# One load of the input on SyncE's queue, or sixteen indexed loads by GpSimd

## The chip, the cores and the metric

The kernel runs on one core of a Trainium2 chip. Its time is the device time of the whole program in microseconds (us), and less is better. The core has TensorE (PE in the profile, with PEld for its weight loads), VectorE (DVE), ScalarE (ACT), GpSimd (POOL) and SyncE (SP), which run side by side, each in the order of its own program, and wait for each other through semaphores. Transfers between the chip's main memory (HBM) and the on-chip memory are issued by one of these engines and carried out by 16 DMA engines. The before kernel took 1201.54, 1200.2 and 1196.77 us in three runs, a median of 1200.2.

## The reference

The program is a decoder of two layers on an input `x` of 8 batches, 256 positions and 128 features in float32, with a context of 8 x 64 rows:

```
x = layernorm(x + attention_16_heads(x))      # causal
x = layernorm(x + linear_cross_attention(x, ctx))
x = layernorm(x + mixture_of_experts_16(x))
x = layernorm(x + gated_recurrence(x))
x = layernorm(x + cross_attention(ctx, x))
x = layernorm(x + mixture_of_experts_64(x))
```

Only the first line matters here. `x` enters it twice: transposed, features on partitions, as the operand of the matrix products, and by rows, positions on partitions, as the term to which the attention's result is added (the residual).

## The kernel before

The 2048 rows of `x` are seen as T = 16 tiles of 128. The host lays them out as `a["x"]`, of shape (128, 16, 128): partition, tile, feature; one partition's data are 8 KB that lie together. On the chip they are held in `X`, a view of `Xp` behind a pad of 256 columns. The transposed copy is `xall`, filled from `a["xT"]`.

SyncE's program (from L374) begins with a row of loads, issued one behind the other without a wait: the context and its weights, the four attention weights `w64v`, `w64o`, `w64q`, `w64k` (512 KB each), `xall` (1 MB, L380), `X` (1 MB, L381), and then the small weights that later stages use.

GpSimd's program (from L417) clears and fills constants, squares a context tile once VectorE has made it (L442), waits for `kn_sum` from VectorE, raises `kn` to the power -0.5 (L444), and enters the main loop. There its part is `divide` (L454), which scales a tile of probabilities by a reciprocal that VectorE has computed.

TensorE first makes context products (L1397, L1404, L1410, L1418) and folds the attention weights into products (L1387, eight groups); ScalarE and VectorE take their results out of PSUM (L627, L871). Then the main loop runs 4 x 16 steps over batches and head pairs. In every step TensorE waits for `Ul`, the low part of a product that VectorE rounds (L940), before it can go on to the scores.

VectorE's order is what counts for the change. Behind its setup stand the clearing of two PSUM banks (L897), the low part of `wq` (L899), the split of the first router's weights (L902, L904), and the wait for `X` (L906). Directly behind that wait the loop begins: `mask_and_max` (L912, L915) reads the scores of the step before, then `Ul` (L940), the copy of the transposed probabilities (L927), in some steps `add_out` (L933), which is the first instruction that reads or writes the data of `X`, and the reciprocals (L922). The waiting instruction is thus ahead of all of VectorE's work of the loop:

```
dve.wait_ge(sem("x_in"), 16)
```

The order is written out by hand for every engine; there is no planner.

Of the kernel before, what the change touches and what calls it, by code (L numbers as in the profile page):

```python
# [19 lines left out]
ACT = mybir.ActivationFunctionType  # L20
AX = mybir.AxisListType
F32 = mybir.dt.float32
# [4 lines left out]
N = B * S  # L27
T = N // 128
# [13 lines left out]
def decoder_program(nc, a, out):  # L42
# [14 lines left out]
    def sb(name, shape, dt=F32, scope=ctx):  # L57
        return scope.enter_context(nc.sbuf_tensor(name, shape, dt))

    with ctx:  # L60
# [13 lines left out]
        cmask = sb("cmask", [128, 2 * 128])  # L74
        ones = sb("ones", [128, 128])
        scratch = sb("scratch", [128, 24])
        st = sb("st", [128, T, 6])
        mv = sb("mv", [128, T, 2])
        rs = sb("rs", [128, T])
# [292 lines left out]
        @block.sync  # L372
        def _(sp):
            sp.dma_start(ctxT[:, :], a["ctxT"]).then_inc(sem("ctx_in"), 16)  # L374
            sp.dma_start(wx[:, :, :], a["wx"]).then_inc(sem("ctx_in"), 16)
            sp.dma_start(brow[:, :], a["brow"]).then_inc(sem("ctx_in"), 16)
            sp.dma_start(bq[:, :], a["bq"]).then_inc(sem("ctx_in"), 16)
            for n in "voqk":
                sp.dma_start(w64[n][:, :, :], a["w64" + n]).then_inc(sem("w_vo_in" if n in "vo" else "w_qk_in"), 16)
            sp.dma_start(xall[:, 0:N], a["xT"]).then_inc(sem("xT_in"), 16)  # L380
            sp.dma_start(X, a["x"]).then_inc(sem("x_in"), 16)  # L381
            sp.dma_start(wr_in[:, :], a["wr0"]).then_inc(sem("wr_in"), 16)
            for name, dst in (("wd", wd_in), ("abias", abias), ("wo1", wo1), ("wqe", wqe), ("wr1", wr1_in),
                              ("ebias", ebias), ("wsh", wsh)):
                sp.dma_start(dst[tuple([slice(None)] * len(dst.shape))], a[name]).then_inc(sem("l1_in"), 16)

            sp.wait_ge(sem("x_added"), NC_)
            sp.dma_start(rw[:, :], a["rw"]).then_inc(sem("rw_in"), 16)
            with sp.Fori(0, E0 // 2) as i:
                for s in range(2):  # L390
                    sp.wait_ge(sem("w_split"), i * 2 + s + 2)
                    sp.dma_start(W0[s][:, :], a["w12"][ds(i * 2 + s, 1), :, :].rearrange("o p n -> p (o n)")).then_inc(sem(f"w_in{s}"), 16)

            sp.wait_ge(sem("r_step"), 8)
            sp.dma_start(decay, wu[:, 0, :]).then_inc(sem("decay_out"), 16)
            sp.wait_ge(sem("decay_out"), 16)
            by_batch = decay.rearrange("(h b) t -> b h t", b=B)
            for g in range(B):
                if g >= 2:
                    sp.wait_ge(sem("scan1_done"), 2 * g - 2)  # L400
                sp.dma_start(Wb[g % 2][:, :].rearrange("p (h t) -> p h t", h=H1),
                             by_batch[g:g + 1, :, :].to_broadcast([128, H1, S])).then_inc(sem(f"decay_in{g % 2}"), 16)

            sp.wait_ge(sem("x_added"), NC_ + NC_)
            with sp.Fori(0, E1 // 4) as i:
                for s in range(2):
                    sp.wait_ge(sem("f_split"), i * 2 + s + 1)
                    sp.dma_start(W3[s][:, :], a["w3"][ds(i * 2 + s, 1), :, :].rearrange("o p n -> p (o n)")).then_inc(sem(f"w_in{s}"), 16)
            for c in range(NC_):
                sp.wait_ge(sem("ln_x"), 5 * T + 4 * c + 4)  # L410
                sp.dma_start(out[:, 4 * c:4 * c + 4, :], X[:, 4 * c:4 * c + 4, :]).then_inc(sem("out_done"), 16)
            sp.wait_ge(sem("out_done"), 16 * NC_)

        @block.gpsimd
        def _(pool):
# [3 lines left out]
            pool.memset(cmask[:, :], 0.0).then_inc(sem("zeroed"), 1)  # L419
            pool.memset(ones[:, :], 1.0).then_inc(sem("consts"), 1)  # L420
            pool.memset(neghalf[:, :], -0.5).then_inc(sem("consts"), 1)
            pool.memset(wrh[:, :].bitcast(F32), 0.0).then_inc(sem("wr_zero"), 1)
            pool.memset(wrl[:, :].bitcast(F32), 0.0).then_inc(sem("wr_zero"), 1)
            pool.wait_ge(sem("zeroed"), 3)
            pool.affine_select(out=ident[:, :], in_=ident[:, :], compare_op=ALU.not_equal, fill=1.0,
                               base=0, pattern=[[-1, 128]], channel_multiplier=1).then_inc(sem("consts"), 1)
# [5 lines left out]
            pool.affine_select(out=blockones[:, :], in_=blockones[:, :], compare_op=ALU.is_ge, fill=0.0,  # L432
                               base=DX - 1, pattern=[[DX, HX], [0, DX]], channel_multiplier=-1).then_inc(sem("consts"), 1)

            pool.memset(xall[:, N:], 0.0).then_inc(sem("x_pad"), 1)
            pool.memset(P[:, 2, :], 0.0).then_inc(sem("norm_done"), 1)
            pool.memset(PT[:, 1, :, :], 0.0).then_inc(sem("pt_done"), 1)
            pool.memset(VO[:, :, :, :], 0.0).then_inc(sem("vo_done"), 1)
# [4 lines left out]
            pool.wait_ge(sem("ctx_dve"), CTX_DVE["kn_sum"])  # L443
            pool.tensor_tensor(kn[:, :], kn[:, :], neghalf[:, 0:B], ALU.pow).then_inc(sem("ctx_pool"), 1)  # L444


            def divide(g, k):

# [169 lines left out]
        def _(act):  # L618
# [12 lines left out]
                               ACT.Copy).then_inc(sem("xh_done"), 1)  # L631

            act.wait_ge(sem("xT_in"), 16)
            act.wait_ge(sem("x_pad"), 1)
            split_x(0, 0)
            act.wait_ge(sem("ctx_pool"), CTX_POOL["kn_done"])
            act.wait_ge(sem("ctx_pe"), CTX_PE["g2_ready"])
# [28 lines left out]


            for c in range(NC_):
                act.wait_ge(sem("q_ready"), c + 1)
                act.activation(EQ[:, c * CH:c * CH + CH], bank(4 + c), ACT.Exp, bias=bq[:, 0:1]).then_inc(sem("q_act"), 1)  # L670

            for c in range(NC_):
                act.wait_ge(sem("q_norm"), c + 1)
                act.activation(RQ[:, c * CH:c * CH + CH], bank(c), ACT.Ln, scale=float(DX)).then_inc(sem("q_act"), 1)
            for c in range(NC_):
                act.wait_ge(sem("q_act"), NC_ + c + 1)
# [111 lines left out]
                act.activation(XTf[:, c * CH:c * CH + CH], bank(c), ACT.Copy).then_inc(sem("ln_hi"), 1)  # L788
            for h in range(2):
                act.wait_ge(sem("es_step"), 6 + 2 * h)  # L790
                act.activation(SE[:, 8 * h:8 * h + 8, :], SE[:, 8 * h:8 * h + 8, :], ACT.Exp).then_inc(sem("e_exp"), 1)
            for c in range(NC_):
                act.wait_ge(sem("e_T"), c + 1)
                act.activation(PE_T[:, c * CH:c * CH + CH], bank(c)[0:64, :], ACT.Copy).then_inc(sem("e_pt"), 1)
            in_turn(lambda c: ln_norm(act, 4, c), lambda c: ln_hi(act, 4, c), 1)

            for c in range(NC_):
# [51 lines left out]

        @block.vector  # L850
        def _(dve):
            dve.wait_ge(sem("consts"), 5)
            dve.memset(sel2[:, 64:72].bitcast(F32), 0.0)
            dve.tensor_tensor(sel2[:, 0:64], ident[:, 0:64], ident[:, 64:128], ALU.add).then_inc(sem("sel2_done"), 1)
            dve.tensor_reduce(halfones[:, :], ident[:, :].rearrange("p (a c) -> p a c", a=2), AX.X, ALU.add).then_inc(sem("halves"), 1)
# [42 lines left out]
            dve.wait_ge(sem("ctx_act"), CTX_ACT["wq_hi"])  # L898
            dve.tensor_tensor(wql[:, :], wx[:, 3, :], wqh[:, :].bitcast(F32), ALU.subtract).then_inc(sem("ctx_dve"), 1)  # L899
            dve.wait_ge(sem("wr_in"), 16)  # L900
            dve.wait_ge(sem("wr_zero"), 2)
            dve.tensor_copy(wrh[:, 0:E0R], wr_in[:, :]).then_inc(sem("ctx_dve"), 1)  # L902
            dve.wait_ge(sem("ctx_dve"), CTX_DVE["wr_split"] - 1)
            dve.tensor_tensor(wrl[:, 0:E0R], wr_in[:, :], wrh[:, 0:E0R].bitcast(F32), ALU.subtract).then_inc(sem("ctx_dve"), 1)  # L904

            dve.wait_ge(sem("x_in"), 16)  # L906

            def mask_and_max(g, k):

# [91 lines left out]
                dve.tensor_tensor(x, x, bank(b), ALU.add).then_inc(sem("x_added"), 1)  # L1001

            def add_query_out(c):
                dve.wait_ge(sem("b_out"), c + 1)
                dve.wait_ge(sem("bo_added"), c + 1)
                add_bank(c, 4 + c)
                dve.wait_ge(sem("x_added"), c + 1)
                ln_stats(dve, 1, c)
# [246 lines left out]
            row_reduce(1, 5, ALU.max)  # L1255
            less_maximum(1, 7)
            for h in range(2):
                dve.wait_ge(sem("e_exp"), h + 1)
                row_reduce(h, 8, ALU.add)
            for h in range(2):  # L1260
                dve.wait_ge(sem("es_step"), 9 + h)
                dve.reciprocal(el[:, 8 * h:8 * h + 8], em[:, 8 * h:8 * h + 8]).then_inc(sem("es_step"), 1)
            for c in range(NC_):
                dve.wait_ge(sem("e_out"), c + 1)
                add_bank(c, 4 + c)
                dve.wait_ge(sem("x_added"), NC_ + c + 1)
                ln_stats(dve, 4, c)
# [106 lines left out]
        def _(pe):  # L1374
# [15 lines left out]


            pe.wait_ge(sem("ctx_in"), 64)
            pe.wait_ge(sem("consts"), 5)
            for n in range(2):
                for p in range(4):
                    dst = bank(n)[:, p * 128:p * 128 + 128]
# [52 lines left out]
                last.then_inc(sem("pv_done"), 1)  # L1449

            pe.wait_ge(sem("fold_lo"), 8)
            pe.wait_ge(sem("consts"), 5)
            pe.wait_ge(sem("acc_free"), 1)
            with pe.Fori(0, B // 2) as i:
                for k in range(STEPS):
# [25 lines left out]
            def project_query(c):  # L1481
                cc = slice(c * CH, c * CH + CH)
                pe.wait_ge(sem("ln_lo"), c + 1)
                mm3(bank(4 + c), (wqh[:, :], wql[:, :]), (XTh[:, cc], XTl[:, cc])).then_inc(sem("q_ready"), 1)

            pe.wait_ge(sem("ctx_dve"), CTX_DVE["wq_lo"])
            in_turn(lambda c: ln_transpose(pe, 0, c), project_query, 2)
            for c in range(NC_):
                pe.wait_ge(sem("q_sq"), c + 1)
                pe.matmul(bank(c), blockones[:, :], SQ[:, c * CH:c * CH + CH], start=True, stop=True).then_inc(sem("q_norm"), 1)  # L1490
            for c in range(NC_):
                pe.wait_ge(sem("q_done"), c + 1)
                for t in tiles(c):
                    dst = bank(4 + c)[:, t % 4 * 128:t % 4 * 128 + 128]
                    last = pe.matmul(dst, Q[:, t * 128:t * 128 + 128], G2[:, t // 2, :], start=True, stop=True)
                last.then_inc(sem("b_out"), 1)


            def gate_logits(c):
# [180 lines left out]
            for t in range(T):  # L1680
                pe.wait_ge(sem("e_prob"), t // 8 + 1)
                last = pe.transpose(bank(t // 4)[0:64, t % 4 * 128:t % 4 * 128 + 128], SE[:, t, :], ident[:, :])
                if t % 4 == 3:
                    last.then_inc(sem("e_T"), 1)
            for t in range(T):
                pe.wait_ge(sem("e_pt"), t // 4 + 1)
                last = pe.matmul(bank(4 + t // 4)[:, t % 4 * 128:t % 4 * 128 + 128], PE_T[:, t * 128:t * 128 + 128], vE[:, t // 2, :],
                                 start=True, stop=True)
                if t % 4 == 3:
                    last.then_inc(sem("e_out"), 1)  # L1690

            def router_logits(c):
                cc = slice(c * CH, c * CH + CH)
# [141 lines left out]
```

## Time and profile before

| | us |
|---|---|
| median of three runs (lowest, highest) | 1200.2 (1196.77, 1201.54) |
| profiled execution: its time | 1198.43 |
| profiled execution: its span, first to last instruction | 1196.7 |
| PE busy | 1059.1 (88%) |
| DVE busy | 886.8 (74%) |
| ACT busy | 678.7 (57%) |
| POOL busy | 426.1 (36%) |
| mean granted TensorE clock, as a share of the full one | 0.922 |

The profile shows one execution, whose time is 1.7 us above its span. Busy shares are means over stages with different limits, so the stretch around the change is to be read by itself: the setup, up to about 35 us, and the start of the main loop, which lasts until about 340 us. Instructions that issue a DMA on SyncE's or GpSimd's queue are not counted as busy; their times stand in the timeline.

### The profile page before, as it was taken

To read this page: it belongs to the slowest core of one execution; us is meant where nothing else is said; L and a number is where in the kernel's file an instruction comes from. 1 tells how busy PE (TensorE), PEld (TensorE's weight loads), DVE (VectorE), ACT (ScalarE), POOL (GpSimd) and SP (SyncE) were. 2 spreads that over 40 slices of the span, in tenths; PEclk is the share of its full clock that TensorE was granted. 3 is DMA by queue.
4 is the path that set the end of the run, shared out by engine and by line. 5 is a ranking of instruction groups with operands and counts; after the bars stand their busy time and mean duration, and the time that the engine had idled before them with its cause. 6 is when DMAs were issued, how large, how long until landed. Compare 5 with 4: busy or idle time off the path is not lost. (4 is left out here: it accounts for less than half of the span.)

```text
span 1196.7 us, 18412 instructions
## 1 busy us (share of the span) xinstructions
PE 1059.1 (88%) x5684; PEld 890.0 (74%) x5684; DVE 886.8 (74%) x2063; ACT 678.7 (57%) x1513; POOL 426.1 (36%) x517
## 2 busy tenths in 40 slices
PE   7899999999966799999897178877869999999995
PEld 7899999999844588888675068875637888888883
DVE  3566666666674789898768599954868888888885
ACT  2666666666665777777688243434634444444444
POOL 3233333333345223232216076753542223222232
PEclk7999999999986899999989578896969999999998
DMA  7000000000000000000000355400000000000000
GB/s 209 1 2 1 0 0 0 0 0 0 0 1 19 18 18 26 18 26 18 1 0 1 62 100 76 48 1 1 28 0 27 20 20 20 21 25 20 20 13 35
DMA packets 18263, 26.70 MB, mean 22 GB/s; under 512 B 1905, under 2 KB 14769, under 8 KB 17714
## 3 DMA queue, kind: packets, MB, share of 16 engines
q1 hardware_dynamic: 18226, 26.24, 10.0%
q8 instruction: 19, 0.31, 0.1%
q14 instruction: 18, 0.15, 0.0%
HBM read 25.12 MB, written 1.11 MB: 22 GB/s over the span
## 5 line engine op out<-in xcount | busy, mean ns | idle before, releaser
L454 POOL TENSOR_TENSOR P<-P,rl 128x256 f32<-128x256 f32 (+1 forms) x130 | 104.8, 827 | 204.9 <-DVE rl L922 204.9
L841 ACT ACTIVATE FG<-PS 128x512 f32<-128x512 f32 x120 | 71.8, 598 | 146.0 <-PE PS L1378 146.0
L915 DVE CUSTOM_DVE_ANT_0 P<-PS,cmask 128x128 f32<-128x128 f32 (+1 forms) x260 | 77.1, 352 | 70.9 <-issue 70.9
L1363 DVE TENSOR_TENSOR FU<-FG,PS 128x512 f32<-128x512 f32 x120 | 82.5, 688 | 49.9 <-PE PS L1378 49.9
L647 ACT ACTIVATE P<-P,mn 128x128 f32<-128x128 f32 (+1 forms) x260 | 114.3, 444 | 2.4 <-DVE mn L915 2.4
L559 POOL TENSOR_TENSOR W3h<-W,ones 128x384 fp32r<-128x384 f32 x32 | 39.3, 1229 | 212.4 <-PE PS L1378 209.6
L704 ACT ACTIVATE SG<-PS 128x512 f32<-128x512 f32 x128 | 76.4, 598 | 46.5 <-PE PS L1378 31.0
L1377 PE MATMUL PS<-XTl,W3h 128*128 128x512 f32 x256 | 101.8, 397 | 0.0
L1376 PE MATMUL PS<-XTh,W3h 128*128 128x512 f32 x256 | 101.3, 396 | 0.4
L1378 PE MATMUL PS<-XTh,W3l 128*128 128x512 f32 x256 | 101.2, 395 | 0.0
L1446 PE MATMUL PS<-VO,PT 128*128 128x128 f32 x804 | 100.6, 275 | 0.0
L1087 DVE TENSOR_TENSOR HL<-Hf,HH 128x512 fp32r<-128x512 f32 x128 | 98.3, 768 | 0.7
L1446 PEld LDWEIGHTS PS<-VO,PT 128*128 128x128 f32 x804 | 95.0, 192 | 0.0
L1346 DVE TENSOR_TENSOR FHL<-FH,FHH 128x512 fp32r<-128x512 f32 x128 | 91.6, 716 | 0.7 <-ACT FHH L831 0.7
L1104 DVE TENSOR_TENSOR Hf<-SG,PS 128x512 f32<-128x512 f32 x112 | 76.8, 685 | 16.5 <-PE PS L1558 16.0
L831 ACT ACTIVATE FHH<-FH 128x512 fp32r<-128x512 f32 x128 | 80.0, 625 | 9.0 <-DVE FH L1355 7.5
L699 ACT ACTIVATE HH<-Hf 128x512 fp32r<-128x512 f32 x128 | 79.7, 623 | 4.0 <-DVE Hf L1092 3.7
L1367 DVE TENSOR_TENSOR FH<-FU,PS 128x512 f32<-128x512 f32 x120 | 81.5, 680 | 0.0
L655 ACT ACTIVATE Uh<-PS 128x512 fp32r<-128x512 f32 x64 | 38.3, 598 | 72.2 <-PE PS L1378 72.2
L927 DVE COPY PT<-PS 128x768 f32<-128x768 f32 x66 | 62.5, 947 | 2.9 <-PE PS L1435 2.9
L1376 PEld LDWEIGHTS PS<-XTh,W3h 128*128 128x128 f32 x256 | 48.1, 188 | 14.8 <-issue 2.9
L1435 PE MATMUL PS<-ident,P 128*128 128x128 f32 x396 | 56.3, 278 | 2.1 <-POOL P L454 2.1
(390 smaller groups left out, 2963.3 us busy)
## 6 DMA issues: line engine op xcount, KB each, us to landing
Wb<-decay SPq DMA_DIRECT2D x8, 1024.0 KB, 14.4
W<-in_w SPq DMA_DIRECT2D x32, 192.0 KB, 2.3
W<-in_w SPq DMA_DIRECT2D x16, 256.0 KB, 2.6
xall<-in_xT SPq DMA_DIRECT2D x1, 1024.0 KB, 13.6
Xp<-in_x SPq DMA_DIRECT2D x1, 1024.0 KB, 15.5
out<-Xp SPq DMA_DIRECT2D x4, 256.0 KB, 2.3
wd_in<-in_wd SPq DMA_DIRECT2D x1, 832.0 KB
w64v<-in_w64v SPq DMA_DIRECT2D x1, 512.0 KB, 6.0
```

The costliest lines, as they stand in the source:

```text
L454: last = pool.tensor_tensor(v, v, f, ALU.mult)
L647: last = act.activation(P[:, slot, c:c + w], P[:, slot, c:c + w], ACT.Exp, scale=-1.0, bias=mn[:, par, q:q + 1], accum_out=ls[:, par, q:q ...
L699: act.activation(HH[:, (k - 1) % 4, :], Hf[:, (k - 1) % 4, :], ACT.Copy).then_inc(sem("hh_done"), 1)
L831: act.activation(FHH[:, (k - 1) % 4, :], FH[:, (k - 1) % 4, :], ACT.Copy).then_inc(sem("fhh_done"), 1)
L1087: dve.tensor_tensor(HL[:, (k - 1) % 4, :], Hf[:, (k - 1) % 4, :], HH[:, (k - 1) % 4, :].bitcast(F32), ALU.subtract).then_inc(sem("hl_done" ...
L1346: dve.tensor_tensor(FHL[:, (k - 1) % 4, :], FH[:, (k - 1) % 4, :], FHH[:, (k - 1) % 4, :].bitcast(F32), ALU.subtract).then_inc(sem("fhl_do ...
L1363: dve.tensor_tensor(FU[:, k % 2, :], FG[:, k % 2, :], bank(6), ALU.mult).then_inc(sem("ft_done"), 1)
L1367: dve.tensor_tensor(FH[:, k % 4, :], FU[:, k % 2, :], bank(7), ALU.mult).then_inc(sem("fh_done"), 1)
L1376: pe.matmul(dst, l[0], r[0], start=start, stop=False, skip_group_check=skip)
L1377: pe.matmul(dst, l[0], r[1], start=False, stop=False, skip_group_check=skip)
L1378: return pe.matmul(dst, l[1], r[0], start=False, stop=stop, skip_group_check=skip)
L1446: last = pe.matmul(OB[:, dst:dst + 128], PT[:, par, h, blk * 128:blk * 128 + 128], VO[:, half, 2 * p + h, :], start=first, stop=(p == PAIR ...
```

## The change

The one load of `X` goes out of SyncE's program. GpSimd makes a table `xrow` of row numbers, in which partition p holds p*16 + t in column t, and behind its work on `kn`, ahead of the main loop, issues sixteen indexed loads. Load t reads from the table one row number for each partition and fetches that row of 512 bytes, so that it fills tile t. VectorE waits in the same place as before, now for all sixteen.

```diff
+        xrow = sb("xrow", [128, T], mybir.dt.uint32)
...
             sp.dma_start(xall[:, 0:N], a["xT"]).then_inc(sem("xT_in"), 16)
-            sp.dma_start(X, a["x"]).then_inc(sem("x_in"), 16)
             sp.dma_start(wr_in[:, :], a["wr0"]).then_inc(sem("wr_in"), 16)
...
-            pool.memset(wrh[:, :].bitcast(F32), 0.0).then_inc(sem("wr_zero"), 1)
-            pool.memset(wrl[:, :].bitcast(F32), 0.0).then_inc(sem("wr_zero"), 1)
+            pool.memset(wrh[:, :].bitcast(F32), 0.0).then_inc(sem("consts"), 1)
+            pool.memset(wrl[:, :].bitcast(F32), 0.0).then_inc(sem("consts"), 1)
...
-            pool.memset(xall[:, N:], 0.0).then_inc(sem("x_pad"), 1)
+            pool.memset(xall[:, N:], 0.0).then_inc(sem("consts"), 1)
+            pool.iota(xrow[:, :], [[1, T]], base=0, channel_multiplier=T).then_inc(sem("x_rows"), 1)
...
             pool.tensor_tensor(kn[:, :], kn[:, :], neghalf[:, 0:B], ALU.pow).then_inc(sem("ctx_pool"), 1)
+            pool.wait_ge(sem("x_rows"), 1)
+            rows = a["x"].rearrange("p t d -> (p t) d")
+            for t in range(T):
+                pool.indirect_dma_start(out=X[:, t, :], out_offset=None, in_=rows,
+                                        in_offset=bass.IndirectOffsetOnAxis(ap=xrow[:, t:t + 1], axis=0)).then_inc(sem("x_in"), 16)
...
-            act.wait_ge(sem("x_pad"), 1)
+            act.wait_ge(sem("consts"), 8)
...
-            dve.wait_ge(sem("consts"), 5)
+            dve.wait_ge(sem("consts"), 7)
...
-            dve.wait_ge(sem("wr_zero"), 2)
+            dve.wait_ge(sem("consts"), 7)
...
-            dve.wait_ge(sem("x_in"), 16)
+            dve.wait_ge(sem("x_in"), 16 * T)
```

The rest of the diff merges semaphores. `wr_zero` and `x_pad` go into `consts`, as shown; `q_ready`, `q_norm` and `b_out`, all raised by TensorE in the second line of the reference, become one `q_pe`; `e_exp` and `e_pt`, raised by ScalarE, become `e_act`, and `e_T` and `e_out`, raised by TensorE, become `e_pe`. Each wait on one of them is for the count that is reached when the same instruction as before has finished.

## Rows read from the trace of the kernel before

**Rows 1.** Busy time by stage: stage and its length in us, busy us of each engine.

```profile
0.00:34.70 34.70, 26.15 (x144) 25.09 (x144) 11.73 (x25) 9.85 (x21) 10.32 (x21) 0.75 0.64 180
34.70:351.00 316.30, 307.80 (x2171) 279.42 (x2172) 210.34 (x848) 205.49 (x683) 116.08 (x150) 0.98 0.00 0
```

**Rows 2.** Timeline, 29 to 38 us: start us, us, what [idle before it].

```profile
29.21 0.27 DVE L893 MEMSET Xp<- 128x256 f32 x1
...
33.25 0.91 DVE L897 MEMSET PS<- 128x1024 f32 x1 [3.18 <-ACT G L640]
34.07 0.27 DVE L899 TENSOR_TENSOR wql<-wx,wqh 128x128 fp32r<-128x128 f32 x1
34.26 0.16 DVE L902 CAST wrh<-wr_in 128x14 fp32r<-128x14 f32 x1
34.46 0.17 DVE L904 TENSOR_TENSOR wrl<-wr_in,wrh 128x14 fp32r<-128x14 f32 x1
34.68 0.06 DVE L912 MEMSET scratch<- 128x1 f32 x1
...
36.59 0.63 PE L1376 MATMUL PS<-NVh,xh 128*128 128x512 f32 x1 [3.00 <-DVE Ul L940]
...
37.57 1.61 POOL L454 TENSOR_TENSOR P<-P,rl 128x256 f32<-128x256 f32 x2 [16.95 <-DVE rl L922]
```

**Rows 3.** Timeline of POOL and SP in the setup.

```profile
4.83 3.51 POOL L438 MEMSET VO<- 128x4096 f32 x1
...
5.15 0.59 SPq L380 DMA_DIRECT2D xall<-in_xT  x1
5.78 0.50 SPq L381 DMA_DIRECT2D Xp<-in_x  x1
6.32 0.43 SPq L382 DMA_DIRECT2D wr_in<-in_wr  x1
...
10.62 1.04 POOL L442 TENSOR_TENSOR csq<-ck 128x512 f32<-128x512 f32 x1 [2.27 <-DVE ck L863]
...
18.97 1.65 POOL L444 TENSOR_TENSOR kn<-kn,neghalf 128x8 f32<-128x8 f32 x1 [7.31 <-DVE kn L875]
```

**Rows 4.** DMA issues of 0 to 80 us: KB, median us from issue to landing.

```profile
xall<-in_xT SPq DMA_DIRECT2D x1, 1024.0 KB, 13.6
Xp<-in_x SPq DMA_DIRECT2D x1, 1024.0 KB, 15.5
...
w64o<-in_w64o SPq DMA_DIRECT2D x1, 512.0 KB, 7.9
...
wr_in<-in_wr SPq DMA_DIRECT2D x1, 7.0 KB, 15.1
```

**Rows 5.** The chain of waits at 667 us: start us, us, what.

```profile
667.03 1.95 DMA decay<-wu
```

**Rows 6.** POOL's instructions by shape: busy us, mean ns of one | idle before.

```profile
L527 POOL TENSOR_TENSOR gb<-gb,dfb 128x1020 f32<-128x1020 f32 x16 | 37.6, 2352 | 55.8 <-ACT dfb L779 55.8
...
L323 POOL TENSOR_TENSOR rs<-ms,neghalf 128x4 f32<-128x4 f32 x24 | 24.9, 1037 | 2.0
...
L501 POOL CAST esel<-sel 128x128 fp32r x16 | 11.1, 694 | 0.0
...
L560 POOL CAST fsel<-sel 128x128 fp32r x30 | 8.6, 286 | 0.0
...
L482 POOL MEMSET scratch<- 128x1 f32 x1 | 0.1, 98 | 0.0
```

**Rows 7.** Who waited for whom, 0 to 80 us: us, times, longest.

```profile
PE PS L1397 <- DMA bq<-in_bq: 5.9, 1, 5.9
...
PE PS L1387 <- DMA w64o<-in_w64o: 1.6, 1, 1.6
```

**Rows 8.** Stages around the loop's start: columns of Rows 1, then granted clock, DMA share, GB/s.

```profile
26.00:30.00 4.00, 4.00 (x20) 3.78 (x19) 2.40 (x5) 1.34 (x3) 0.00 (x0) 0.50 0.00 0
...
36.00:37.00 1.00, 0.41 (x1) 0.33 (x2) 1.00 (x2) 0.93 (x4) 0.00 (x0) 0.91 0.00 0
37.00:38.00 1.00, 1.00 (x4) 0.78 (x3) 0.49 (x2) 0.00 (x0) 0.43 (x1) 0.50 0.00 0
...
40.00:41.00 1.00, 1.00 (x9) 1.00 (x9) 0.96 (x8) 0.10 (x1) 0.00 (x0) 0.89 0.00 0
41.00:42.00 1.00, 1.00 (x11) 1.00 (x10) 0.71 (x3) 1.00 (x4) 0.00 (x0) 1.00 0.00 0
```

**Rows 9.** Busy time of the stretch in which the new loads begin, columns of Rows 8.

```profile
20.60:34.70 14.10, 12.99 (x74) 12.46 (x72) 7.03 (x15) 5.35 (x14) 0.02 (x1) 0.67 0.25 91
```

More of the change, by code:

```diff
@@ L668, in _ @@
             for c in range(NC_):
-                act.wait_ge(sem("q_ready"), c + 1)
+                act.wait_ge(sem("q_pe"), c + 1)
                 act.activation(EQ[:, c * CH:c * CH + CH], bank(4 + c), ACT.Exp, bias=bq[:, 0:1]).then_inc(sem("q_act"), 1)
             for c in range(NC_):
-                act.wait_ge(sem("q_norm"), c + 1)
+                act.wait_ge(sem("q_pe"), NC_ + c + 1)
                 act.activation(RQ[:, c * CH:c * CH + CH], bank(c), ACT.Ln, scale=float(DX)).then_inc(sem("q_act"), 1)
@@ L790, in _ @@
                 act.wait_ge(sem("es_step"), 6 + 2 * h)
-                act.activation(SE[:, 8 * h:8 * h + 8, :], SE[:, 8 * h:8 * h + 8, :], ACT.Exp).then_inc(sem("e_exp"), 1)
+                act.activation(SE[:, 8 * h:8 * h + 8, :], SE[:, 8 * h:8 * h + 8, :], ACT.Exp).then_inc(sem("e_act"), 1)
             for c in range(NC_):
-                act.wait_ge(sem("e_T"), c + 1)
-                act.activation(PE_T[:, c * CH:c * CH + CH], bank(c)[0:64, :], ACT.Copy).then_inc(sem("e_pt"), 1)
+                act.wait_ge(sem("e_pe"), c + 1)
+                act.activation(PE_T[:, c * CH:c * CH + CH], bank(c)[0:64, :], ACT.Copy).then_inc(sem("e_act"), 1)
             in_turn(lambda c: ln_norm(act, 4, c), lambda c: ln_hi(act, 4, c), 1)
@@ L1003, in add_query_out @@
             def add_query_out(c):
-                dve.wait_ge(sem("b_out"), c + 1)
+                dve.wait_ge(sem("q_pe"), 2 * NC_ + c + 1)
                 dve.wait_ge(sem("bo_added"), c + 1)
@@ L1257, in _ @@
             for h in range(2):
-                dve.wait_ge(sem("e_exp"), h + 1)
+                dve.wait_ge(sem("e_act"), h + 1)
                 row_reduce(h, 8, ALU.add)
@@ L1263, in _ @@
             for c in range(NC_):
-                dve.wait_ge(sem("e_out"), c + 1)
+                dve.wait_ge(sem("e_pe"), NC_ + c + 1)
                 add_bank(c, 4 + c)
@@ L1392, in _ @@
             pe.wait_ge(sem("ctx_in"), 64)
-            pe.wait_ge(sem("consts"), 5)
+            pe.wait_ge(sem("consts"), 7)
             for n in range(2):
@@ L1451, in _ @@
             pe.wait_ge(sem("fold_lo"), 8)
-            pe.wait_ge(sem("consts"), 5)
+            pe.wait_ge(sem("consts"), 7)
             pe.wait_ge(sem("acc_free"), 1)
@@ L1483, in project_query @@
                 pe.wait_ge(sem("ln_lo"), c + 1)
-                mm3(bank(4 + c), (wqh[:, :], wql[:, :]), (XTh[:, cc], XTl[:, cc])).then_inc(sem("q_ready"), 1)
+                mm3(bank(4 + c), (wqh[:, :], wql[:, :]), (XTh[:, cc], XTl[:, cc])).then_inc(sem("q_pe"), 1)
             pe.wait_ge(sem("ctx_dve"), CTX_DVE["wq_lo"])
@@ L1489, in _ @@
                 pe.wait_ge(sem("q_sq"), c + 1)
-                pe.matmul(bank(c), blockones[:, :], SQ[:, c * CH:c * CH + CH], start=True, stop=True).then_inc(sem("q_norm"), 1)
+                pe.matmul(bank(c), blockones[:, :], SQ[:, c * CH:c * CH + CH], start=True, stop=True).then_inc(sem("q_pe"), 1)
             for c in range(NC_):
@@ L1495, in _ @@
                     last = pe.matmul(dst, Q[:, t * 128:t * 128 + 128], G2[:, t // 2, :], start=True, stop=True)
-                last.then_inc(sem("b_out"), 1)
+                last.then_inc(sem("q_pe"), 1)
             def gate_logits(c):
@@ L1683, in _ @@
                 if t % 4 == 3:
-                    last.then_inc(sem("e_T"), 1)
+                    last.then_inc(sem("e_pe"), 1)
             for t in range(T):
-                pe.wait_ge(sem("e_pt"), t // 4 + 1)
+                pe.wait_ge(sem("e_act"), 2 + t // 4 + 1)
                 last = pe.matmul(bank(4 + t // 4)[:, t % 4 * 128:t % 4 * 128 + 128], PE_T[:, t * 128:t * 128 + 128], vE[:, t // 2, :],
@@ L1689, in _ @@
                 if t % 4 == 3:
-                    last.then_inc(sem("e_out"), 1)
+                    last.then_inc(sem("e_pe"), 1)
             def router_logits(c):
```

## The prediction

> **What bounds the kernel now.** I read the stages first. The setup takes 34.7 us. In the attention loop behind it TensorE is busy for 307.8 of 316.3 us while GpSimd has 116.1 us of work [rows 1]. So what reaches the end of the program is TensorE's time, and a later start of the loop is a later end of everything: at 97% busy the loop has no gaps in which TensorE could catch up.
>
> Second, the timeline at the seam, to see what releases the loop. VectorE finishes the split of the router's weights at 34.46 + 0.17 = 34.63 us and begins the loop's first instruction, L912, at 34.68. There is nothing between them: the wait for `X` stands at exactly this place and cost nothing, since `X` had landed at 5.78 + 15.5 = 21.3 us [rows 2 to 4]. TensorE had run out of work and sat idle for 3.0 us until VectorE gave it `Ul` at 36.59 [rows 2]. So at this seam VectorE is the engine on the path, and `X` has a slack of 34.68 - 21.3 = 13.4 us. How late may `X` be? Until 34.68 us for nothing; from there each us of lateness is a us of VectorE, hence of TensorE, hence of the end. That the data are first needed much later, at `add_out`, helps nothing, since the wait is ahead of the loop.
>
> Third, GpSimd's own row of work. Its setup is over at 18.97 + 1.65 = 20.62 us, and it then idles 16.95 us until its first `divide` at 37.57 [rows 2, 3]. The sixteen loads go into this hole. The hole as a whole is 17 us, but what counts is when the last load has landed.
>
> **The change part by part.**
>
> Removed: one issue of 0.50 us on SP and 1 MB from the queue. The loads landed nearly in the order of their issue: `xall` at 5.15 + 13.6 = 18.8, `X` at 21.3, `wr_in` behind it at 6.32 + 15.1 = 21.4 [rows 3, 4]. `X` thus took about 2.5 us of the queue behind everything the setup needs. Later loads come up to 2.5 us earlier, but VectorE reads `wr_in` only at 34.26 [rows 2], 12.8 us after it landed. Gain: 0. The only waits of TensorE for a DMA in the setup are 5.9 us for `bq`, issued ahead of `X`, and 1.6 us for `w64o` [rows 7], which landed at 11.2 us. If `X`, issued at 5.78, shared bandwidth with `w64o`, part of the 1.6 us could come back; that is the bound of the gain, -1.6 us. I take 0, since `X` landed behind the 3.7 MB issued ahead of it.
>
> Added, the table: one iota of 128x16. No iota is in the trace. It stands in front of memsets that end at 4.83 + 3.51 = 8.3 us, and POOL then idles 2.27 us until 10.62 [rows 3]. Even at 1.65 us, the pow over 8 columns and the longest instruction on so few columns, it is inside the idle time. Cost 0; without that cover at most 1.65 us.
>
> Merged semaphores: GpSimd does its instructions in order and each merged count is reached by the same instruction as before. Cost 0; no cover is needed.
>
> Added, the sixteen indexed loads. They begin when POOL is free, at 20.62 us. Let c be the time that POOL spends on one of them, and let the last take 1.95 us from its issue to its semaphore, which is the row of a small transfer that someone waits for [rows 5]. Then `X` is complete at 20.62 + 16c + 1.95, and the loop is late by
>
> D = 20.62 + 16c + 1.95 - 34.68 = 16c - 12.1 us, and 0 where that is below 0.
>
> No row shows c, so it is bounded. From below, SP's issue of a plain load, 0.43 us [rows 3]: 16 x 0.43 = 6.9, D = 0. A gain is excluded but for the 1.6 us above. From above, the longest kind of POOL instruction in the whole trace, 2.35 us on 1020 columns [rows 6]: 16 x 2.35 = 37.6, D = 25.5. Between them lie the pow instructions on few columns, 1.04 us for 4 and 1.65 us for 8 [rows 3, 6]. An indexed load must have GpSimd read 128 row numbers and make a transfer of each, which is more like such an instruction, long for its size, than like an SP issue that says the whole transfer in one step. I take their mean, 1.3 us (an estimate; the middle of the two ends, 1.39, is near it). 16 x 1.3 = 20.8, `X` complete at 43.4, D = 8.7 us. The point that decides: c = 0.76 us gives D = 0, c = 1.13 us gives D = 6.0, which is 0.5%.
>
> The page DMA: Bandwidth & Descriptors of the Trainium skill (Latency and other measured facts) puts the first byte of a DMA issued by GpSimd at about 1 us, which it calls the emission overhead of the cores; by it c would be 1.0, D = 3.9 and the time 1202.3. No row of this trace can check it, as GpSimd issues no DMA here; it names no indexed load of 128 separate rows.
>
> Does something queued behind the loads make it worse? POOL's next instruction is the first `divide`. It needs `rl`, which VectorE makes behind the wait, so it moves to 37.57 + 8.7 = 46.3; POOL has issued its last load at 41.4. It is not late. ScalarE waits for VectorE's minima and TensorE for `Ul`, both moved by D and no more.
>
> TensorE's clock: it idles 3.0 us now and would idle 11.7. After the 3.0 us the granted clock fell to 0.50, its 1.2 GHz level, and the first matmuls of the loop took 0.63 us; at 41 us it was back at 1.00 [rows 2, 8]. After a longer idle the same restart has to be gone through, from the same low level. I count 0. If it took twice as long, some 3.5 us more at half the clock, up to 1.7 us.
>
> VectorE's hold on GpSimd: the same POOL cast of 128x128 takes 286 ns in one stage and 694 ns in another [rows 6], so POOL can be slowed by its neighbours. While the loads begin VectorE is busy 7.0 of 14.1 us [rows 9]; once it waits for `X` it is idle. The bound is that POOL stands still for those 7.0 us; the instructions that copy or clear on-chip data in one stream are L893 and L902, 0.43 us [rows 2]. I take 0, and count up to 1 us for it in the range.
>
> The page SBUF — State Buffer of the Trainium skill (SBUF: two separate sides) says that GpSimd can't write descriptors while VectorE runs a two-port instruction such as a plain copy; by it the sum would grow by those 0.43 us at most, to 1207.5. The unequal casts agree with some such hold but don't show which instructions cause it.
>
> Sum: 0 + 0 + 8.7. Against the profiled execution: 1198.43 + 8.7 = 1207.1 us. That execution lies 1.8 us under the median of the runs; from the median it is 1208.9. I forecast 1208.
>
> **The rivals.**
>
> A, the other side: the issues are cheap and the wait is not, or hardly, felt. Its place is the same wait; it holds from c at or below 1.13 us. For it: 17 us of idle POOL are covered whatever happens, and SP issues a load in 0.43 to 0.59 us [rows 2, 3]. Against it: the index table has to be read and 128 rows handled apart. With c = 0.95, D = 3.1: 1201.5; with c up to 0.76 nothing: 1198.4.
>
> B, the loads are much dearer than one ordinary POOL instruction. If each must land before the next is issued, c = 0.43 + 1.95 = 2.4 us, D = 26: 1224. For it: one semaphore counts all sixteen, and I see no row of many loads out of POOL. Against it: SP issues eighteen loads in a row without waiting for any. If POOL handled the 128 rows one after another at the price of its smallest instruction, 0.098 us [rows 6], c = 12.5 us, D = 188: 1386. Against it: the other POOL instructions handle 128 partitions at once.
>
> The page GPSIMD Engine Reference of the Trainium skill (Performance pitfalls for Q7 kernels) warns of just this, one small read per gather index at about 102 cycles each; at its 1.2 GHz an estimate from it is 10.9 us a load and a time near 1361. Nothing in this trace shows it.
>
> C, faster: the queue without `X` delivers `w64o` earlier, at most -1.6 us, and c is under 0.66 so that `X` isn't late even then: 1196.8. That is inside what counts as no change.
>
> D, the change does not do what it says: the loads could start earlier or later than 20.6. They can't start earlier, since they stand behind the wait for `kn_sum` in POOL's program; a code load ahead of the first would add once. ScalarE's table load at the start of the trace is not of this kind, so I bound it by one long POOL instruction, 2.35 us; it lies within my range.
>
> **How the numbers follow.** The forecast case (c from 1.13 to 2.35, plus small additions) gets 0.50; A 0.36; B 0.11, of which 0.03 for the row-by-row form; C 0.03. What a measurement of this kernel can tell from no change is about 0.5%, 6 us. Slower by more: forecast case and B, 0.61. Within: A and nearly all of C, 0.37. Faster by more: 0.02. The range: at the low end 1200, c = 0.86 from the profiled execution, which leaves out the cheaper half of A and C, some 0.13; at the high end 1227, which takes in the upper bound of c with 2 us of small additions and leaves out 0.07 of B.
>
> **What would show it.** In the new trace: POOL's sixteen issues from about 20.6 us, each 1.3 us long, end near 41.4; the last of `X` lands near 43.4; L912 starts there instead of at 34.68 and its idle time is put down to the DMA; TensorE idles 11 to 12 us ahead of its first matmul on `Ul`; from there to the end the length is unchanged within 2 us. Wrong if L912 still starts near 34.7 (A), if the issues are spaced over 2.3 us (B), or if later stages change length.

## The result, and the profile after

The changed kernel took 1208.31 us (median of four runs, 1206.98 to 1210.07) against 1200.2 for the kernel before, whose fourth run, at 2063.41 us, counts as slow and is left out. The ratio is 1.0075, 95% interval 1.0053 to 1.0098: slower by 8 to 9 us of 1200. The forecast was 1208. The profiled execution has a span of 1205.2 us, 8.5 more than that of before.

By stages, the columns of [rows 1], the changed kernel's start of the loop having moved from 34.7 to 43.05 us:

```profile
0.00:34.70 34.70, 26.16 (x144) 25.09 (x144) 10.36 (x20) 8.88 (x19) 21.13 (x33) 0.75 0.63 169
34.70:43.05 8.35, 0.00 (x0) 0.00 (x0) 1.34 (x4) 1.09 (x3) 5.05 (x5) 0.61 0.16 47
43.05:351.00 307.95, 300.81 (x2149) 276.52 (x2150) 202.58 (x831) 198.24 (x670) 111.76 (x146) 0.98 0.00 0
```

The setup holds the same 26.2 us of TensorE as before [rows 1]. Behind it a stretch of 8.35 us has come in which TensorE does nothing at all. GpSimd's timeline shows what it did in the meantime (start, duration; first and last of sixteen loads, and the first `divide`):

```profile
18.98 1.65 POOL L445 TENSOR_TENSOR kn<-kn,neghalf 128x8 f32<-128x8 f32 x1 [7.46 <-DVE kn L882]
20.83 1.23 POOL L451 DMA_INDIRECT Xp<-in_x,xrow  x1 [0.19 <-issue]
22.36 0.95 POOL L451 DMA_INDIRECT Xp<-in_x,xrow  x1 [0.30 <-issue]
...
36.12 1.26 POOL L451 DMA_INDIRECT Xp<-in_x,xrow  x1 [0.31 <-issue]
...
40.18 0.95 POOL L451 DMA_INDIRECT Xp<-in_x,xrow  x1 [0.30 <-issue]
45.94 1.61 POOL L461 TENSOR_TENSOR P<-P,rl 128x256 f32<-128x256 f32 x2 [4.81 <-DVE rl L929]
```

One load is 0.95 us and 0.30 us of nothing behind it, so 1.25 us from one to the next. The last ends at 41.13. VectorE's timeline, to be held against [rows 2]:

```profile
35.48 0.91 DVE L904 MEMSET PS<- 128x1024 f32 x1 [5.39 <-ACT G L647]
36.30 0.27 DVE L906 TENSOR_TENSOR wql<-wx,wqh 128x128 fp32r<-128x128 f32 x1
36.48 0.16 DVE L909 CAST wrh<-wr_in 128x14 fp32r<-128x14 f32 x1
36.68 0.17 DVE L911 TENSOR_TENSOR wrl<-wr_in,wrh 128x14 fp32r<-128x14 f32 x1
43.05 0.06 DVE L919 MEMSET scratch<- 128x1 f32 x1 [6.20 <-DMA Xp<-in_x,xrow]
```

The first instruction of the loop starts at 43.05, 1.92 us behind the end of the last issue, and waited 6.20 us for the DMA. But the lines above it start 2.2 us later than in [rows 2], before the wait is reached, and that was not forecast. ScalarE and TensorE show more of it:

```profile
33.01 2.18 ACT L647 ACTIVATE G<-PS,kn 128x128 f32<-128x128 f32 x8 [4.54 <-remote]
40.70 0.60 ACT L662 ACTIVATE Uh<-PS 128x512 fp32r<-128x512 f32 x1 [5.51 <-remote]
```

```profile
29.74 0.83 PE L1425 MATMUL PS<-wx,GBT 128*128 128x128 f32 x6
...
31.32 0.28 PE L1385 MATMUL PS<-xh,Ml 128*128 128x256 f32 x1
...
44.96 0.79 PE L1383 MATMUL PS<-NVh,xh 128*128 128x512 f32 x1 [11.36 <-DVE Ul L947]
```

`G` needs L1425, which ended at 30.58, and starts at 33.01. `Uh` needs the product that ended at 31.60, and starts at 40.70. "remote" means that the wait was ended by a semaphore update which the profile can't assign to an instruction near it. In the kernel before the two started at 30.79 and 32.80, within 0.1 us of their inputs or of ScalarE's own work.

Granted clock: before, one stretch at half, of about 3.4 us, from 36.8 to 40.2 [rows 8]; now it lasts from about 36.6 to 50.2 us:

```profile
37.00:40.00 3.00, 0.00 (x0) 0.00 (x0) 0.00 (x0) 0.00 (x0) 2.27 (x3) 0.50 0.15 44
...
46.00:50.00 4.00, 4.00 (x16) 3.61 (x15) 1.20 (x9) 0.75 (x2) 1.55 (x2) 0.50 0.00 0
50.00:51.00 1.00, 1.00 (x10) 1.00 (x9) 0.52 (x1) 1.00 (x4) 0.00 (x0) 0.90 0.00 0
```

The delay followed through the timelines: 8.4 us at the loop's start, 9.1 at the first `add_out` (47.59 to 56.69), 9.3 at the end of the loop (first normalization 335.34 to 344.65), 8.5 at the end of the span.

### The profile page after: what moved, and what is told of

Same layout as the page of the kernel before. It is cut to its first block and busy times, and to the rows that moved or that the text cites. A ratio compares the mean times of both kernels' runs of the same rounds, so it can differ in the third digit from the quotient of the medians.

```text
span 1205.2 us, 18428 instructions
## 1 busy us (share of the span) xinstructions
PE 1061.3 (88%) x5684; PEld 892.4 (74%) x5684; DVE 887.5 (74%) x2063; ACT 679.6 (56%) x1513; POOL 442.2 (37%) x534
## 5 line engine op out<-in xcount | busy, mean ns | idle before, releaser
L711 ACT ACTIVATE SG<-PS 128x512 f32<-128x512 f32 x128 | 76.8, 601 | 48.7 <-PE PS L1385 32.4
L1111 DVE TENSOR_TENSOR Hf<-SG,PS 128x512 f32<-128x512 f32 x112 | 76.7, 684 | 18.5 <-PE PS L1565 17.6
L1383 PEld LDWEIGHTS PS<-XTh,W3h 128*128 128x128 f32 x256 | 48.0, 188 | 13.6 <-issue 2.9
```

The costliest lines, as they stand in the source:

```text
L1383: pe.matmul(dst, l[0], r[0], start=start, stop=False, skip_group_check=skip)
```

## The experiments

All but two are compared in time with the kernel before. For each, three marks of its profiled execution: the start of `kn`, of the loop's first VectorE instruction, and of the first `add_out`. The setup itself comes in two forms, with `kn` at 18.5 to 19.3 us or at 20.3 to 20.8, whatever the kernel (in e10_early `kn` stands behind the loads, and the rest of its setup is of the later form); the low-clock stretch differs too. So each is read against the undisturbed kernel of its own form, before or e1_merges.

| kernel | ratio, interval | kn | loop | add_out |
|---|---|---|---|---|
| before | 1 | 18.97 | 34.68 | 47.59 |
| after | 1.0075, 1.0053 to 1.0098 | 18.98 | 43.05 | 56.69 |
| e1_merges | 1.0004, 0.9991 to 1.0017 | 20.69 | 36.93 | 48.33 |
| e2_late_wait | 1.0081, 1.0063 to 1.0099 | 20.57 | 39.27 | 55.08 |
| e3_half_rows | 1.0106, 1.0088 to 1.0124 | 20.81 | 45.89 | 59.73 |
| e8_eight | 1.0029, 1.0017 to 1.0042 | 20.81 | 38.27 | 51.81 |
| e4_plain_pool | 0.9952, 0.9936 to 0.9969 | 20.32 | 36.57 | 47.97 |
| e5_one_plain_pool | one run, 1203.3 us | 20.60 | 36.24 | 49.15 |
| e6_sp16 | one run, 1199.1 us | 18.94 | 34.88 | 47.78 |
| e7_spread | 1.0025, 1.0005 to 1.0044 | 18.83 | 37.61 | 50.71 |
| e9_plain_32 | 1.0027, 0.9998 to 1.0057 | 19.32 | 35.27 | 48.26 |
| e13_plain_32_wait | 1.0059, 1.0043 to 1.0075 | 20.78 | 41.16 | 54.69 |
| e10_early | 0.9997, 0.9983 to 1.0010 | 28.84 | 36.71 | 49.62 |
| e11_four_late | 1.0036, 1.0025 to 1.0047 | 18.45 | 34.70 | 52.74 |

**The merged semaphores alone.**

```diff
# against the changed kernel
+            sp.dma_start(X, a["x"]).then_inc(sem("x_in"), 16)
-            pool.iota(xrow[:, :], ...)
-            for t in range(T): pool.indirect_dma_start(...)
```

> The changed kernel with its one plain load of X back on SyncE's queue and without index table and indexed loads: only the merged semaphores are left of the change. My theory: the merges cost nothing, ratio 1.000 and the loop's first VectorE instruction at 34.7 us. Rival (the merged counts are reached later, or cost the engines time): up to the whole 1.0075, with a later start of the loop or a longer second line of the reference.

The ratio is 1.0004. VectorE begins the loop at 36.93, not at the forecast 34.7, but `kn` was itself 1.7 us late, and nothing of the change stands ahead of it. By `add_out` the kernel is only 0.7 us behind the kernel before, as TensorE's clock has no low stretch at the loop's start here. The merges show no cost; the interval (0.9991 to 1.0017) leaves room for 2 us at most. This kernel is the mark for the others with the later setup.

**The wait moved to the first use.**

```diff
-            dve.wait_ge(sem("x_in"), 16 * T)
...
             def add_out(b, g):
+                dve.wait_ge(sem("x_in"), 16 * T)
                 dve.wait_ge(sem("pv_done"), g + 1)
```

> All sixteen indexed loads as in the change, but VectorE waits for them only ahead of add_out, its first use of X (47.6 us in the kernel before). My theory (the wait's place turns the loads into time): the 8.4 us go. What is late next is the first divide, behind the last load at 41.1 us: it ends at 42.7 instead of 39.2, and TensorE's second group of transposes starts at about 42.8 instead of 40.6, so about +2 us, ratio 1.002. Rival R (the loads hold up ScalarE: in the changed kernel Uh starts at 40.70 us although its input was ready at 31.6): Uh still starts at 40.7, TensorE's first matmul on NVh at 42 instead of 36.6, +5.4 us, ratio 1.0045. Rival N (the loads disturb nothing and divide has slack): ratio 1.000.

My theory failed: the ratio is 1.0081, as large as with the wait in front. Rival R is seen, though it had been priced at 1.0045. TensorE's product was there at 33.97, and ScalarE and VectorE:

```profile
35.37 2.18 ACT L647 ACTIVATE G<-PS,kn 128x128 f32<-128x128 f32 x8 [5.31 <-issue]
41.76 0.60 ACT L662 ACTIVATE Uh<-PS 128x512 fp32r<-128x512 f32 x1 [4.22 <-remote]
```

```profile
39.27 0.06 DVE L918 MEMSET scratch<- 128x1 f32 x1
...
42.39 0.69 DVE L947 TENSOR_TENSOR Ul<-PS,Uh 128x512 fp32r<-128x512 f32 x1 [1.87 <-issue]
45.36 0.96 DVE L933 COPY PT<-PS 128x768 f32<-128x768 f32 x1 [2.27 <-remote]
```

The loop's VectorE work starts without `X`, and then runs into late signals: `Uh` 7.8 us behind its input, and the copy of the transposes, which TensorE had finished at 34.6, at 45.36. By `add_out` the kernel is 6.8 us behind e1_merges. Two causes lie over each other in the changed kernel, and taking the wait away frees nothing that the time shows.

**Half the rows, half the loads.**

```diff
# e3_half_rows: 16 indexed loads of 64 partitions; the others by SP
-   out=X[:, t, :], ... ap=xrow[:, t:t + 1]
+   out=X[0:64, t, :], ... ap=xrow[0:64, t:t + 1]
# e8_eight: 8 indexed loads of 128 partitions; tiles 0 to 7 by SP
-   for t in range(T):
+   for t in range(T // 2, T):
```

> Sixteen indexed loads of 64 rows instead of 128; the other 64 partitions come by one plain load on SyncE's queue. My theory (the price is of the load, not of the row): spacing of the loads still 1.25 us, the loop starts at 43 us, ratio 1.0075. Rival (the price is of the row): spacing near 0.6 to 0.8 us, last landing at 32 to 35 us, the loop starts at 34.7 to 36, ratio 1.000 to 1.001.

> Eight indexed loads of 128 rows for tiles 8 to 15; tiles 0 to 7 come by one plain load on SyncE's queue. My theory (late = issue start + n x 1.25 + 1.9 us): the last lands at 20.8 + 10 + 1.9 = 32.7 us, before VectorE gets to the wait, ratio 1.000. Rival R (GpSimd's loads hold up ScalarE): VectorE gets to the wait late, as in the changed kernel at 36.9 instead of 34.6, +2 us, ratio 1.002. Rival (a fixed delay of using this kind of load at all): most of the 8.4 us stays, ratio 1.005 or more.

Issues of 64 rows, and of 128 in the second kernel (minimum, median, maximum in ns):

```profile
L452 POOL DMA_INDIRECT Xp<-in_x,xrow x16: 902/907/1172, 22.6 to 41.1; - x16
```

```profile
L452 POOL DMA_INDIRECT Xp<-in_x,xrow x8: 943/946/1230, 22.6 to 31.7; - x8
```

Half the rows save 39 ns of 946: the price is of the load, as expected. But the kernel with 64 rows isn't as slow as the changed one, it is slower (1.0106), since `G` waited until 41.93 us for a product that was done at 33.1. With eight loads the last recorded landing is at 34.29 us, ahead of any wait for them, and the time still rose by 3.5 us (1.0029), against a forecast of nothing:

```profile
34.30 2.18 ACT L648 ACTIVATE G<-PS,kn 128x128 f32<-128x128 f32 x8 [4.01 <-remote]
```

TensorE had ended at 32.41. `G` is 1.9 us late and starts as the last load lands. The loop starts 1.3 us behind that of e1_merges and reaches `add_out` 3.5 us behind it, with TensorE's clock at half until 45.2 us, which it isn't there. Rival R again, and no fixed price of 8 us.

**Plain loads by GpSimd and by SyncE.**

```diff
# e4: pool.dma_start(X[:, t, :], a["x"][:, t, :]) for the 16 tiles
# e5: pool.dma_start(X, a["x"]), once
# e6: sp.dma_start(X[:, t, :], a["x"][:, t, :]) for the 16 tiles, at the old place
```

> Sixteen plain loads of one tile each by GpSimd, in the same place, no index table. My theory (the price is that of GpSimd issuing a load, indexed or not): spacing 1.0 to 1.25 us, the loop starts between 39 and 43 us, ratio 1.004 to 1.0075. Rival (the price is the indexing: 128 row numbers read and handled): spacing near SyncE's 0.5 us, last landing at 31, ratio 1.000.

> One plain load of the whole of X (1 MB) by GpSimd in the same place. My theory (the number of issues is the price): one issue of 1 to 3 us at 20.8, landed by about 27 us, the loop starts at 34.7, time within 2 us of the kernel before. Rival (GpSimd's queue is slow in moving the bytes): X lands after 34.7 us and the loop is late.

> Sixteen plain loads of one tile each on SyncE's queue where the one load stood. My theory (only the engine that issues matters here, since SyncE's issues have 13 us of slack): sixteen issues of 0.4 to 0.5 us, done at about 13.5, all landed by 23 us, the loop starts at 34.7, within 2 us of the kernel before. Rival (the rows of 512 bytes are the price, whoever asks): X lands after 34.7 us and the loop is late.

```profile
L447 POOL DMA_DIRECT2D Xp<-in_x x16: 537/537/782, 21.9 to 30.1; - x16
```

A plain issue by GpSimd takes 0.54 us and has no gap behind it, against 0.95 and 0.30 for an indexed one: the rival is right, the indexing is more than half the price. Sixteen of them are landed by 32.4 us and nothing is late. Its ratio of 0.9952 would make it faster than both kernels by 0.5%, but its profiled execution reaches `add_out` only 0.4 us ahead of e1_merges, and I found no mechanism for the rest; the single load by GpSimd (landed in 5.6 us) and SyncE's sixteen stood near the kernel before, as expected. I don't claim the gain.

**Spread over the idle time, and all of it early.**

```diff
# e7_spread: loads 0 and 1 ahead of csq, 2 to 6 between csq and kn, 7 to 15 behind kn
# e10_early: all 16 behind the memsets, then kn; csq by VectorE
+            for t in range(T): pool.indirect_dma_start(...)
-            pool.tensor_tensor(csq[:, :, :], ck[:, :, :], ck[:, :, :], ALU.mult)
             pool.tensor_tensor(kn[:, :], kn[:, :], neghalf[:, 0:B], ALU.pow)
```

> The sixteen indexed loads spread over GpSimd's idle time in the setup: two ahead of csq, five between csq and kn, nine behind kn. My theory (late = last issue's end + 1.9 us, 1.25 us for each): two loads run 8.5 to 11.0, so csq starts at 11.0 instead of 10.6 with 5 us of slack; five end near 18.3, ahead of kn at 19; nine end at 20.8 + 11.25 = 32.0, landed at 34.0, before VectorE gets to the wait at 34.6. The 8.4 us go: ratio 1.000 to 1.001. Rival R (loads hold up ScalarE): VectorE gets to the wait 2 us or more late, ratio 1.002 or more. Rival (loads beside the 3.7 MB of setup loads slow those): w64o lands later than 11.2 us and the whole setup is late by that.

> All sixteen indexed loads right behind GpSimd's memsets, from 8.7 us, with csq moved to VectorE and kn behind the loads. By my theory of two causes (VectorE's wait, and TensorE's signals held back while indexed loads are in flight after about 30 us) both end: the last issue ends at 28.7, landed at 30.6, kn at 30.4, G starts at 30.8 to 31.5 if the setup runs as in the kernel before, the loop at 34.7 to 35.5, ratio 1.000 to 1.001. Rival (indexed loads cost TensorE's signals time wherever they are): the folds of the attention weights or kn are late by 2 us or more, ratio 1.002 or more.

Spread, the last issue ends at 31.8 us and the wait costs nothing, but `G` starts at 33.72 instead of the 30.79 of before, 1.9 us behind the end of the last issue and 0.5 us behind the last recorded landing, and the loop 2.9 us late: 1.0025. Early, the loads run from 8.66 to 28.81 us, among TensorE's folds, and neither these nor `G` wait:

```profile
29.28 3.44 PE L1424 MATMUL PS<-wx,GBT 128*128 128x128 f32 x16
```

```profile
32.82 2.18 ACT L644 ACTIVATE G<-PS,kn 128x128 f32<-128x128 f32 x8 [2.53 <-PE PS L1424]
34.83 0.65 ACT L659 ACTIVATE Uh<-PS 128x512 fp32r<-128x512 f32 x1
```

TensorE ends at 32.72, `G` starts at 32.82, and the ratio is 0.9997. The sixteen indexed loads show no cost in this place (the interval reaches 1.0010): neither their number nor their bytes are the price.

**Are plain loads in flight as harmful? And indexed ones beside the running loop?**

```diff
# e9: 32 plain loads of half a tile by GpSimd, VectorE's wait moved to add_out
# e13: the same loads, the wait ahead of the loop as in the changed kernel
# e11: 4 indexed loads behind this wait, 12 tiles by SP, VectorE's wait in add_out
+            pool.wait_ge(sem("u_lo"), 1)
```

> Thirty-two plain loads of half a tile each by GpSimd, in the place of the sixteen indexed ones, and VectorE's wait for them only ahead of add_out. At the 0.54 us of a plain issue they are in flight until about 40 us, beside the loop's start, as the indexed ones were. Theory H1 (any load of GpSimd's in flight holds back TensorE's signals from about 30 us on): ScalarE's G and Uh start 2 us or more after TensorE's end, VectorE's Ul as late as 40 us, ratio 1.004 or more. Theory H2 (only the indexed ones do): G starts within 0.2 us of TensorE's end, Uh right behind it, the loop begins at 34.7 to 37 us, ratio 1.000 to 1.003.

> The thirty-two plain loads of the run before, which left TensorE's signals prompt, now with VectorE's wait in the changed kernel's place, ahead of the loop. My theory (the wait's place turns a late landing into time, with nothing held back): Uh is done by 34 to 35.5 us, VectorE idles from about 35 us until the last landing at 40 to 41.5 us, L912's counterpart starts there, and by add_out the kernel is 5 to 6 us behind the kernel before, ratio 1.004 to 1.006. Rival (only the held signals cost time, the wait is harmless): ratio as with the late wait, within 0.001 of 1.0027, and the loop starts by 37 us.

> Four indexed loads (tiles 12 to 15), issued only after VectorE's first Ul, at 36.6 us, so beside the running loop; tiles 0 to 11 come by one plain load on SyncE's queue; VectorE waits only ahead of add_out. GpSimd's first divide starts at about 41.8 instead of 37.6. Theory H2 (TensorE's signals are held back while indexed loads are in flight, until the last has landed at about 43.7): the next Uh and VO copies of ScalarE start late, VO at 43 instead of 38.1, the loop falls back by 4 to 6 us in this stretch, ratio 1.004. Rival (the signals are held only while TensorE is idle or at the loop's entry): VO starts within 0.2 us of TensorE's end, and only the late divide is seen, 2 to 3 us, ratio 1.002.

In e9 the plain loads are issued from 20.9 to 38.1 us, as long as the indexed ones were, and TensorE's signals are prompt: L1421 ends at 31.28, `G` starts at 31.38. H2 is right on the signals. The ratio of 1.0027 has an interval that reaches 0.9998, and I found no cause for it. In e13 the same loads are waited for ahead of the loop:

```profile
41.16 0.06 DVE L915 MEMSET scratch<- 128x1 f32 x1 [4.09 <-DMA Xp<-in_x]
```

```profile
35.15 0.65 ACT L658 ACTIVATE Uh<-PS 128x512 fp32r<-128x512 f32 x1
```

`Uh` was done at 35.8, VectorE waits for the DMA until 41.16, TensorE's low-clock stretch comes back, and `add_out` is 6.4 us behind e1_merges, of which 4.2 are the loop's later start: 1.0059. Here is the forecast's mechanism by itself, without late signals. It is the traces that show it: the ratios of e13 and e9 were taken against different runs of the kernel before, and their intervals overlap. In e11 the four indexed loads run from 36.86 to 41.84 beside TensorE's work, and `VO` and `Uh` start within 0.1 us of their inputs, at 37.62 and 40.27:

```profile
40.27 0.60 ACT L664 ACTIVATE Uh<-PS 128x512 fp32r<-128x512 f32 x1 [2.06 <-PE PS L1388]
```

The rival is right on the signals. What costs time there is the late `divide`, for which TensorE idles 3.29 us, and the clock, which stays at half until 48.35 us (1.0036, more than the rival's 1.002). So indexed loads in flight don't hold the signals back at all times, though these were only four.

## Why the prediction was right, and where it was not

**The price of a load.** Forecast 1.3 us between two loads, bounded by 0.43 and 2.35; it is 1.25. The sum of the changed kernel's own numbers: 20.83 + 15 loads to the last issue at 40.18, + 0.95, + 1.92 to the wait's end, 43.05. The landing had been taken as 1.95 us [rows 5]. D came out as 8.4 instead of 8.7. The choice of the pow rows [rows 3, 6] as the nearest was luck in part: the busy time of 0.95 lies below both, and the 0.30 us of gap was in no row.

**The wait as the place.** Shown by e13: a late landing ahead of the loop is paid in full, plus the clock. Shown by e10 as well: landed by 30.5 us, the loads cost nothing. Queued work behind the loads (`divide`) was not late, as forecast.

**Not forecast: late signals.** The step "ScalarE waits for VectorE's minima and TensorE for `Ul`, both moved by D and no more" failed. While indexed loads are in flight around the entry of TensorE's loop, `G` and `Uh` start long after their inputs: 2.4 and 9.1 us in the changed kernel, up to 11.6 in e3. In the changed kernel this is hidden under the wait for the most part, as `Uh` ends at 41.3 and the wait at 43.05. That is why the sum held, and it is luck: nothing in the forecast said that a second delay would fit under the first. The formula's zero for loads that land in time fails for the same reason: e8 and e7 landed in time and still lost 3 us. And a reader who had followed the forecast to its obvious remedy, the wait at the first use, would have gained nothing (e2).

**The clock.** Taken as 0, bound 1.7 us. The low stretch grew from 3.4 to 13.6 us, of which 5.2 fall on work (44.96 to 50.2) instead of 3.4. From the loop's start to its end 0.9 us are lost beyond D, which is what 1.8 us more at half the clock cost. By the end of the span the difference is back at 8.5; later stages differ by that much between executions.

**VectorE against GpSimd.** Bound 7 us, taken as 0. Fourteen of the sixteen issues took 0.94 or 0.95 us, the first 1.23. The thirteenth, at 36.12, took 1.26 while VectorE ran L906 and the cast L909; in e2 the thirteenth, at 37.71, took 2.03 beside the same instructions and the first ones of the loop, which there don't wait. The Trainium skill, page SBUF — State Buffer (SBUF: two separate sides), has VectorE's plain copies lock GpSimd out of writing descriptors; the trace agrees with some such hold of 0.3 to 1.1 us, about the 1 us that the range had counted for it, though memsets of VectorE at 29.2 to 30.1 lengthened nothing. It doesn't show which instruction holds.

**Semaphore merges, iota, `X` off SyncE's queue:** nothing that shows, as forecast (e1 for the merges; the iota took 0.15 us in idle time; the setup's TensorE work is 26.16 us against 26.15).

**Open.** What holds TensorE's signals is not settled. The trace also records when a semaphore is raised, and this narrows it down. In e7 four signals of TensorE, for `G`, for `Uh`, for the copy of the transposes and for the weighted sums, are recorded at 33.63, 33.71, 33.79 and 33.91 us, while their last matmuls are placed at 30.50, 31.46, 32.12 and 33.46. In the kernel before the same four come at 30.71, 31.61, 32.27 and 33.61, each within 0.02 us of its matmul. The six transposes between the second and the third take 0.66 us there and can't have been done within 0.08. So TensorE's work was done, and its semaphores were held and let go in a row. ScalarE's signal was not held in the changed kernel: L904 starts 0.29 us behind the last `G`, as in the kernel before. Loading of code is not the cause either: from 24 to 50 us the changed kernel's DMA record has GpSimd's queue alone:

```profile
q0 software_dynamic: 480, 0.98, 13.2%
```

Runs show the conditions: indexed and not plain (e9), around the loop's entry and not among the folds (e10) or in the loop (e11, four loads), released about when the last load lands (e7, e8) or partly before it (the changed kernel, e2, e3).

One rival is untested, and it is the recording itself. In the five kernels with late signals, and in no other, the trace has lost records of semaphores in this stretch: of the 256 increments of `x_in`, 64 are left in the changed kernel, and the profile gives no landing time for its loads. In e10 and e11 all are there:

```profile
Xp<-in_x,xrow POOLq DMA_INDIRECT x16
```

```profile
Xp<-in_x,xrow POOLq DMA_INDIRECT x16, 5.5
```

The first line is of the changed kernel, the second of e10_early. Late signals and lost records go together in every kernel here. Whether one causes the other, or both come from a third thing, no run shows, nor whether the signals would be late with nothing recorded.

## What to carry to other kernels

The landing of a load counts from the wait's place in program order, not from the first use, and GpSimd's indexed loads cost 1.25 us each for 128 rows and 1.21 for 64, so give them fewer instructions or an earlier place. Moving the wait is no remedy when the same loads also delay others: first check that the engines beside it start right behind their inputs. And when a forecast's sum is right, still compare the lines that should not have moved; here they showed a second delay of about the same size.

## What was not expected of the hardware

- An indexed load of GpSimd occupies it 0.95 us for 128 rows and 0.91 us for 64, with 0.30 us of gap behind each; the first took 1.23. A plain one takes 0.54 with no gap.
- With indexed loads in flight around the loop's entry, instructions that waited for TensorE started 1.9 to 11.6 us late in five kernels (after, e2, e3, e7, e8), and in none with plain loads in flight (e4, e9, e13). In the same five the trace lost semaphore records.
- TensorE's signals came in a row when they came: four within 0.28 us in e7, where the kernel before took 2.9 us for them.
- The granted clock was at half for 13.6 us (36.6 to 50.2) with TensorE idle from 33.6 to 44.96, and for 3.4 us (36.8 to 40.2) with TensorE idle from 33.59 to 36.59. In e1_merges TensorE idled 2.39 us in this place, and the clock stayed full.
